# Last quarter of a selective scan: nine of 64 state products made by TensorE and ScalarE instead of VectorE and GpSimd, on one Trainium2 core

## The chip, the cores and the metric

One core of a Trainium2 chip runs the whole program in one launch. The metric is the device time of one launch in microseconds (us); below, a time is the median of repeated launches, and the span is what the profiler shows of one launch from its first to its last instruction. The engines have their own instruction queues and are tied together by semaphores: TensorE (PE in the rows, PEld its weight loads), VectorE (DVE), ScalarE (ACT), GpSimd (POOL) and SyncE (SP), which issues most DMAs.

## The reference

A layer of attention, a mixture of experts, then a bidirectional Mamba block on 4 sequences of 256 positions, and a gated feed-forward block. The change is in the Mamba block, of which this is the core:

```python
def step(h, inp):
    dt_t, B_t, C_t, x_t = inp
    dA = jnp.exp(dt_t[..., None] * A)
    h = dA * h + (dt_t * x_t)[..., None] * B_t[:, None, :]
    y = jnp.einsum('bds,bs->bd', h, C_t)
    return (h, y)
```

There are DI = 512 channels d and DS = 16 states s. The output y is then multiplied with silu(z) and goes through a projection.

## The kernel before

The Mamba block (function `mamba`) treats four segments: a direction (two forward, then two backward) times half of the 1024 positions (HALF = 512, two sequences). A segment has 64 steps (SSTEP), in two pairs of channel blocks with 32 steps (PSTEP) each, so there are 256 steps and eight pairs, numbered 0 to 7. A step is one block of 128 channels (two blocks take turns) and one state s, over 512 positions. Steps are named here by their place in the pair: step 17 of pair 6 is n = 6 * 32 + 17 = 209. The last segment is pairs 6 and 7.

A step goes through five engines:

- GpSimd multiplies u with the row B for two steps at once (line 2119, "uB"), three such pairs ahead at most (UPAIRS).
- ScalarE writes exp(dt * A) into a PSUM bank (lines 2222 and 2223, tile `da` or `side`). Which bank a step gets is worked out by `banks`: three banks `da`, and the bank `S1` (tile name `side`) where `spare` says that nothing else needs it. In the last segment `spare` is true throughout, so four banks go round, and step n's exp waits until step n-4 has been read.
- VectorE runs the recurrence (`tensor_tensor_scan`): in place in the bank (line 2339), or, where GpSimd makes the product, into one of four buffers hS (line 2336).
- The product with the row C is made by VectorE (line 2238, 20 of 32 steps, called V steps here), one step behind the scan, or by GpSimd (line 2129, 12 of 32 steps, P steps: 1, 3, 5, 8, 10, 12, 15, 17, 19, 22, 24, 26). GpSimd's product of step m stands in its queue behind the uB of steps m+4 and m+5. It has three output buffers, and waits until TensorE has added the product three before.
- TensorE adds the products in PSUM (`ya0`, `ya1`; lines 2360 and 2364). In pairs 0 to 6 the sum is kept turned, so an add is four transposes of 128x128; a copy (line 1739), `sum_back` and VectorE's gate (line 2250) follow at step 4 of the next pair. In pair 7 the sum isn't turned, and an add is one matmul of 512 columns (two passes).

All five queues are written out by hand and are strictly in order. Beside the steps each engine has a side program (`side_tensor`, `side_scalar`, `side_vector`), a generator that yields the step at which its next piece is due: `side.advance(step)` issues all that is due. On TensorE the step given is the index of the add in the order of `summed` (a P step's add comes four places late) plus AHEAD = 2. In the last segment TensorE's side program has the dt matmuls of block 2 (due 2) and 3 (due 17), their sums (`sum_tensor`, due 10 and 22), the output projection of the segment before (due 18 and 30) and the first half of its own (due 48). ScalarE's has abs and relu (due 9 and 23), exp (11, 24), ln (12, 25) and the copy of dt (`keep_dt`, 20 and 31), then eight table copies (34 to 48), each issued after the exp of that step. `dt_tensor` of block 3 waits for `keep_dt` of block 2, and `sum_tensor` for the ln of its block, since they share banks.

At a segment's beginning ScalarE loads another table, makes silu(z) and loads the first table again (lines 1775 and 1933). After the last scan VectorE makes three table pieces (line 2020), the two gates of pair 7, five more pieces and the two output sums (line 2025); TensorE makes the second half of the projection (line 1624) as the gates come.

Of the kernel before, what the change touches and what calls it, by code (L numbers as in the profile page):

```python
# [24 lines left out]
P = 128  # L25
# [5 lines left out]
HALF = 512  # L31
# [29 lines left out]
DB = DI // P  # L61
# [1213 lines left out]
UPAIRS, CBUF, PBUF, DABUF, HBUF = 3, 4, 3, 3, 4  # L1275
# [31 lines left out]

def on_pool(n):

    return n % PSTEP % 7 in (1, 3, 5) and n % PSTEP < PSTEP - LATE  # L1310


def pool_steps(n):

    full, part = divmod(n, PSTEP)
    return full * sum(on_pool(i) for i in range(PSTEP)) + sum(on_pool(i) for i in range(part))


def vector_steps(n):
    return n - pool_steps(n)  # L1320
# [74 lines left out]
def mamba(c, g, dram, wt, ws, acc, hh, hl, xn, sc, first_weights):  # L1395
# [25 lines left out]
    s_dd, s_yt, s_yb = map(sem, "dd yt yb".split())  # L1421
    s_da, s_ub, s_sc, s_hv, s_hp, s_av, s_ap, s_sk, s_g, s_om, s_oa = map(
# [3 lines left out]
    with ExitStack() as ctx:  # L1426
# [18 lines left out]
        def read(e, n):  # L1445

            if on_pool(n):
# [180 lines left out]

        def dt_tensors(e, k):
# [14 lines left out]
        def side_tensor(e, seg):  # L1644
            k = seg + 1
# [86 lines left out]
        def copy_sum(e, pair, b):  # L1732
# [3 lines left out]
            e.wait_ge(s_ap, pool_steps(last))  # L1736
            if pair:
# [268 lines left out]
        def side_scalar(e, seg):  # L2006
            own = first_scalar(e) if seg == 0 else middle_scalar(e, seg) if seg < NSEG - 1 else last_scalar(e)
            return in_turn(sums_scalar(e, seg), own)
# [57 lines left out]
        with nc.Block() as block:  # L2066
# [25 lines left out]
            def _(e):  # L2092
# [11 lines left out]
                for r in range((STEPS + LATE) // 2):  # L2104
# [17 lines left out]
                    for m in (2 * r - LATE, 2 * r - LATE + 1):  # L2122
                        if m >= 0 and on_pool(m):
# [5 lines left out]
                            e.tensor_tensor(hP[:, k % PBUF, :], hS[:, k % HBUF, :], RC[:, row % CROWS, :],  # L2129
# [3 lines left out]
            def _(e):  # L2133
# [66 lines left out]
                for n in range(STEPS):  # L2200
# [13 lines left out]
                    elif BANK[n] == DABUF:  # L2214
                        e.wait_ge(s_dtc, DB * (seg + 1) + 1)
                    to, first = by_seq(states[BANK[n]][:, :]), 0 if seg < 2 else SEQ - 1
# [3 lines left out]
                    stays = past is not None and on_pool(past) and place(past)[0] // 2 == seg // 2  # L2220
# [6 lines left out]
                    side.advance(n % SSTEP)  # L2227
                side.finish()

            @block.vector  # L2230
            def _(e):
# [9 lines left out]
                def gate(pair, b):  # L2241

                    last, seg, d = (pair + 1) * PSTEP, pair // 2, 2 * (pair % 2) + b
                    if pair == LASTPAIR:
                        e.wait_ge(s_av, vector_steps(last - 1 + b))
                        e.wait_ge(s_ap, pool_steps(last))
                    else:
# [71 lines left out]
                for n in range(STEPS):  # L2319
# [12 lines left out]
                    if on_pool(n):  # L2332
                        k = pool_steps(n)
                        if k >= HBUF:
                            e.wait_ge(s_hp, k - HBUF + 1)
# [5 lines left out]
                    if n and not on_pool(n - 1):  # L2341
# [565 lines left out]
```

## Time and profile before

| | us |
|---|---|
| median of 3 launches | 930.74 (930.12 to 931.51) |
| profiled launch | 922.39 |
| span in the profile | 920.7 |
| PE, DVE, ACT, POOL busy | 759.4, 762.6, 541.6, 658.8 |
| VectorE's last product ends | 843.4 |

The scans run from about 430 to 843 us of the span. The profiled launch was itself 8.4 us shorter than the median; differences worked out on its span are added to the median. An engine that is busy for nearly all of a stretch isn't yet its bound: what each waits for, and how short the waits are, has to be read from the timelines.

### The profile page before, as it was taken

To read this page: it belongs to the slowest core of one execution; us is meant where nothing else is said; L and a number is where in the kernel's file an instruction comes from. 1 tells how busy PE (TensorE), PEld (TensorE's weight loads), DVE (VectorE), ACT (ScalarE), POOL (GpSimd) and SP (SyncE) were. 2 spreads that over 40 slices of the span, in tenths; PEclk is the share of its full clock that TensorE was granted. 3 is DMA by queue.
4 is the path that set the end of the run, shared out by engine and by line. 5 is a ranking of instruction groups with operands and counts; after the bars stand their busy time and mean duration, and the time that the engine had idled before them with its cause. 6 is when DMAs were issued, how large, how long until landed. Compare 5 with 4: busy or idle time off the path is not lost. (4 is left out here: it accounts for less than half of the span.)

```text
span 920.7 us, 13477 instructions
## 1 busy us (share of the span) xinstructions
PE 759.4 (82%) x3802; PEld 492.4 (53%) x3802; DVE 762.6 (83%) x1261; ACT 541.6 (59%) x1303; POOL 658.8 (72%) x454
## 2 busy tenths in 40 slices
PE   4889977899999994797879579787879766877998
PEld 2466654466666662344555455445645554422786
DVE  3588867678889985848989999999999999999843
ACT  1588855444444442476777887677775785652332
POOL 3177853477777883229999989999999999995000
PEclk9899999799999998898989799999999988799999
DMA  4000008599879844414565565656557665552001
GB/s 117 1 1 1 0 1 336 216 414 328 300 275 355 298 146 154 128 47 134 156 169 185 160 153 152 190 158 175 142 163 192 155 173 155 164 157 58 1 1 46
DMA packets 67347, 141.77 MB, mean 154 GB/s; under 512 B 12688, under 2 KB 23312, under 8 KB 65104
## 3 DMA queue, kind: packets, MB, share of 16 engines
q1 hardware_dynamic: 56432, 117.62, 42.2%
q0 software_dynamic: 6048, 18.59, 5.7%
q10 hardware_dynamic: 4800, 4.78, 1.6%
q8 instruction: 28, 0.46, 0.2%
q14 instruction: 39, 0.32, 0.1%
HBM read 129.92 MB, written 11.04 MB: 153 GB/s over the span
## 5 line engine op out<-in xcount | busy, mean ns | idle before, releaser
L2119 POOL TENSOR_TENSOR uB<-u,rows_B 128x1024 f32<-128x1024 f32 x127 | 297.9, 2354 | 0.0
L2339 DVE TENSOR_TENSOR_SCAN da<-da,uB 128x512 f32<-128x512 f32 x145 | 175.1, 1220 | 11.8 <-ACT da L2223 9.9
L2364 PE MATMUL ya<-ident,hV 128*128 128x128 f32 x560 | 96.2, 302 | 49.7 <-DVE hV L2238 49.6
L2129 POOL TENSOR_TENSOR hP<-hS,rows_C 128x512 f32<-128x512 f32 x96 | 121.7, 1268 | 8.3 <-PE ya L2364 3.9
L2364 PEld LDWEIGHTS ya<-ident,hV 128*128 128x128 f32 x560 | 71.4, 153 | 102.1 <-DVE hV L2238 76.3
L2336 DVE TENSOR_TENSOR_SCAN hS<-da,uB 128x512 f32<-128x512 f32 x86 | 103.6, 1204 | 6.2 <-issue 2.6
L1232 PE MATMUL gups<-wring,xT 128*128 128x448 f32 x252 | 105.8, 542 | 0.0
L1140 POOL DMA_INDIRECT xg<-x_rows,li x63 | 71.9, 1142 | 38.7 <-issue 14.6
L2238 DVE TENSOR_TENSOR hV<-da,rows_C 128x512 f32<-128x512 f32 x145 | 96.8, 668 | 0.7 <-DMA rows_C<-bc_rows 0.7
L1147 POOL DMA_INDIRECT y_rows<-y,yi x63 | 72.1, 1145 | 21.4 <-issue 17.1
L2222 ACT ACTIVATE da<-zero 128x2 f32<-128x2 f32 x145 | 25.0, 173 | 102.0 <-DVE hV L2238 101.1
L1069 DVE SCALAR_TENSOR_TENSOR lutw<-eq,lutb,lutw 128x865 f32<-128x865 bf16 x75 | 83.5, 1113 | 0.0
L2223 ACT ACTIVATE da<-dt,fm_A 128x510 f32<-128x510 f32 x123 | 81.7, 674 | 0.0
L372 POOL TENSOR_TENSOR prob<-prob,ri 128x1024 f32<-128x1024 f32 x32 | 60.6, 1893 | 22.9 <-DVE ri L535 22.9
L2223 ACT ACTIVATE da<-dt,bm_A 128x510 f32<-128x510 f32 x108 | 71.6, 674 | 0.0
L606 ACT ACTIVATE prob<-sps,mx 128x256 f32<-128x256 f32 x128 | 58.9, 478 | 7.3 <-DVE mx L531 7.2
L1232 PEld LDWEIGHTS gups<-wring,xT 128*128 128x128 f32 x252 | 47.8, 191 | 27.5 <-issue 24.1
L2364 PEld LDWEIGHTS ya<-ident,hP 128*128 128x128 f32 x336 | 44.0, 150 | 23.1 <-issue 21.1
L2364 PE MATMUL ya<-ident,hP 128*128 128x128 f32 x336 | 54.6, 288 | 0.0
L881 ACT ACTIVATE y<-yps 128x256 f32<-128x256 f32 x63 | 24.2, 384 | 47.7 <-DMA y_rows<-y,yi 31.9
L531 DVE TENSOR_REDUCE mx<-sps 128x4 f32<-128x1024 f32 x32 | 39.1, 1221 | 13.8 <-PE sps L436 12.8
L1487 PE MATMUL side<-raw,conv_diag 128*128 128x512 f32 x72 | 38.6, 619 | 5.1 <-ACT side L1703 5.1
(429 smaller groups left out, 1733.6 us busy)
## 6 DMA issues: line engine op xcount, KB each, us to landing
rows_B<-bc_rows SPq DMA_DIRECT2D x128, 256.0 KB, 3.6
rows_C<-bc_rows SPq DMA_DIRECT2D x128, 256.0 KB, 4.3
wring<-in_moe_own SPq DMA_DIRECT2D x31, 704.0 KB, 5.8
wring<-in_moe_two SPq DMA_DIRECT2D x16, 1024.0 KB, 14.3
rows_sum<-y_rows SPq DMA_DIRECT2D x6, 512.0 KB, 8.3
lut_i<-in_lut_idx SPq DMA_DIRECT2D x1, 2160.0 KB, 8.4
x<-in_x SPq DMA_DIRECT2D x4, 256.0 KB, 3.4
x_rows<-xnw ACTq DMA_DIRECT2D x1, 1024.0 KB, 14.4
```

The costliest lines, as they stand in the source:

```text
L372: e.tensor_tensor(prob[:, u % NP, :, :], prob[:, u % NP, :, :], ri[:, u, :].unsqueeze(2).broadcast_to([P, GROUPS, SEQ]), ALU.mult).then_in ...
L1069: e.scalar_tensor_tensor(part, eq[:, n % 4, 0:LCH], g.lutb[:, l:l + 1], part, ALU.mult, ALU.add).then_inc(s_ad, 1)
L1140: e.indirect_dma_start(xg[:, t % XG, :], None, dram["xs"], bass.IndirectOffsetOnAxis(ap=li[:, t:t + 1], axis=0)).then_inc(s_xg[t % XG], 16)
L1147: e.indirect_dma_start(dram["ys"], bass.IndirectOffsetOnAxis(ap=ri[:, t:t + 1], axis=0), y[:, t % YB, :], None).then_inc(s_sc[t % YB], 16)
L1232: mm = e.matmul(gups[:, t % 2, 0:BOTH], xT[:, t % 2, k * P:(k + 1) * P], both[k], start=k == 0, stop=k == KC - 1)
L2119: e.tensor_tensor(uB[:, r % UPAIRS, :, :], u[:, d:d + 2, :], RB[:, r % BROWS, :].unsqueeze(1).broadcast_to([P, 2, HALF]), ALU.mult).then_i ...
L2129: e.tensor_tensor(hP[:, k % PBUF, :], hS[:, k % HBUF, :], RC[:, row % CROWS, :], ALU.mult).then_inc(s_hp, 1)
L2223: e.activation(to[:, :, rest], by_seq(dt[:, d, :])[:, :, rest], ACT.Exp, scale=ws[seg // 2].A[:, d, r % DS:r % DS + 1]).then_inc(s_da, 2 i ...
L2238: e.tensor_tensor(hV[:, k % CBUF, :], states[BANK[n]][:, :], RC[:, r % CROWS, :], ALU.mult).then_inc(s_hv, 1)
L2336: e.tensor_tensor_scan(hS[:, k % HBUF, way], a[:, way], uB[:, r % UPAIRS, b, way], 0.0, ALU.mult, ALU.add).then_inc(s_sc, 1)
L2339: e.tensor_tensor_scan(a[:, way], a[:, way], uB[:, r % UPAIRS, b, way], 0.0, ALU.mult, ALU.add).then_inc(s_sc, 1)
L2364: mm = e.matmul(ya[n % 2][:, part], at[:, part], g.ident[:, :], start=False, stop=False, is_transpose=True, skip_group_check=True)
```

## The change

A third kind of step, A, is made by neither VectorE nor GpSimd. Its scan goes to an hS buffer. TensorE turns the four 128x128 parts into the bank S1 (`turn_state`), ScalarE copies them out with a per-partition scale, the turned C (`scale_state`: four activations of 128x128), and TensorE adds the result: with one matmul in pair 6, whose sum is turned already, with four transposes in pair 7. The kinds of all steps are now strings. Pairs 0 to 5 keep theirs. Pair 6 has A at 10, 14, 19, 25, P at 1, 3, 5, 8, 12, 16, 18, 21, 23, 27 and 18 V steps; pair 7 has A at 3, 9, 13, 19, 23, P at 1, 5, 7, 11, 15, 17, 21, 24, 26, 28 and 17 V steps.

B and C are turned once, near the end of the third segment (`turn_rows`, `keep_rows`, due 62). Since S1 is now used for turning, `spare` is true in the last segment only for steps 0 to 6. TensorE's side program is advanced, in all eight pairs, by the step at whose turn the add is issued rather than by its index in the order. The buffer of B and C moves (`bcr`), the hS count covers P and A steps, and both gates of pair 7 wait for A adds too.

```diff
-UPAIRS, CBUF, PBUF, DABUF, HBUF = 3, 4, 3, 3, 4
+UPAIRS, CBUF, PBUF, DABUF, HBUF, TBUF = 3, 4, 3, 3, 4, 2
+SCALED, ADDED = 3, 6
+KINDS = ["VPVPVPVVPVPVPVVPVPVPVVPVPVPVVVVV"] * (2 * NSEG - 2) + ["VPVPVPVVPVAVPVAVPVPAVPVPVAVPVVVV",
+                                                                "VPVAVPVPVAVPVAVPVPVAVPVAPVPVPVVV"]
...
     seg, m = divmod(n, SSTEP)
     if seg == NSEG - 1:
-        return True
+        return m < 7
...
-    order = []
-    for n in range(pair * PSTEP, (pair + 1) * PSTEP):
-        if not on_pool(n):
-            order.append(n)
-        if n - LATE >= pair * PSTEP and on_pool(n - LATE):
-            order.append(n - LATE)
+    first, order = pair * PSTEP, []
+    for n in range(first, first + PSTEP + LATE):
+        if n < first + PSTEP and not on_pool(n):
+            order.append((n, False))
+        if n - LATE >= first and on_pool(n - LATE):
+            order.append((n - LATE, True))
+        if n - ADDED >= first and turned(n - ADDED):
+            order.append((n - ADDED, True))
...
+        def turn_rows(e):
+            yield 62
+            e.wait_ge(s_bcc, NSEG)
+            e.wait_ge(s_dtc, DB * (NSEG - 1) + 1)
+            for q in range(HALF // P):
+                mm = e.transpose(S1[:, q * 2 * DS:(q + 1) * 2 * DS], sc.bcr[:, q * P:(q + 1) * P],
+                                 g.ident[0:2 * DS, 0:2 * DS])
+            mm.then_inc(s_tb, 1)
+        def keep_rows(e):
+            yield 62
+            e.wait_ge(s_tb, 1)
+            e.activation(sc.bT[:, :, :].rearrange("p q s -> p (q s)"), S1[:, 0:HALF // P * 2 * DS],
+                         ACT.Copy).then_inc(s_bt, 1)
+        def turn_state(e, n):
+            k, i = kept_steps(n), turned_steps(n)
+            e.wait_ge(s_sc, n + 1)
+            if i:
+                e.wait_ge(s_hs, i)
...
+            for q in range(HALF // P):
+                part = slice(q * P, (q + 1) * P)
+                mm = e.transpose(S1[:, part], hS[:, k % HBUF, part], g.ident[:, :])
+            mm.then_inc(s_ht, 1)
+        def scale_state(e, n):
+            i, at = turned_steps(n), DS + n // 2 % DS
+            e.wait_ge(s_ht, i + 1)
+            if i >= TBUF:
+                e.wait_ge(s_at, i - TBUF + 1)
+            for q in range(HALF // P):
+                part = slice(q * P, (q + 1) * P)
+                a = e.activation(sc.hT[i % TBUF][:, part], S1[:, part], ACT.Identity, scale=sc.bT[:, q, at:at + 1])
+            a.then_inc(s_hs, 1)
...
                     side.advance(n % SSTEP)
+                    if n >= SCALED and turned(n - SCALED):
+                        scale_state(e, n - SCALED)
...
-                    if n // PSTEP == LASTPAIR:
+                    if (n // PSTEP == LASTPAIR) != is_turned:
...
-                        if on_pool(n):
+                        if turned(n) and not late:
+                            turn_state(e, n)
+                        elif turned(n):
+                            k = turned_steps(n)
+                            e.wait_ge(s_hs, k + 1)
+                            add(n, sc.hT[k % TBUF][:, :], s_at, True)
+                        elif on_pool(n):
...
-                        side.advance(pair % 2 * PSTEP + i + AHEAD)
+                        side.advance((n + (0 if not late else LATE if on_pool(n) else ADDED)) % SSTEP + AHEAD)
```

## Rows read from the trace of the kernel before

**Rows 1.** Stretches: length, busy PE, PEld, DVE, ACT, POOL; clock, DMA share, GB/s.
```profile
750.00:800.00 50.00, 36.59 (x169) 25.14 (x168) 49.83 (x57) 30.26 (x66) 49.75 (x28) 0.80 0.60 161
800.00:850.00 50.00, 39.05 (x82) 13.88 (x80) 48.96 (x58) 20.73 (x45) 40.36 (x23) 1.00 0.42 116
```

**Rows 2.** Groups of instructions, 730 to 850 us: busy, mean ns of one.
```profile
L2119 POOL TENSOR_TENSOR uB<-u,rows_B 128x1024 f32<-128x1024 f32 x34 | 79.6, 2350 | 0.0
L2129 POOL TENSOR_TENSOR hP<-hS,rows_C 128x512 f32<-128x512 f32 x26 | 32.9, 1265 | 0.2 <-DVE hS L2336 0.2
```

**Rows 3.** VectorE's timeline: start, us, line (idle before, releaser).
```profile
756.77 1.20 DVE L2336 TENSOR_TENSOR_SCAN hS<-da,uB 128x512 f32<-128x512 f32 x1
757.89 0.66 DVE L2238 TENSOR_TENSOR hV<-da,rows_C 128x512 f32<-128x512 f32 x1
758.47 1.22 DVE L2339 TENSOR_TENSOR_SCAN side<-side,uB 128x512 f32<-128x512 f32 x1
...
829.84 1.22 DVE L2336 TENSOR_TENSOR_SCAN hS<-da,uB 128x512 f32<-128x512 f32 x1 [0.61 <-ACT da L2223]
```

**Rows 4.** GpSimd's timeline, same stretch.
```profile
827.40 4.65 POOL L2119 TENSOR_TENSOR uB<-u,rows_B 128x1024 f32<-128x1024 f32 x2
```

**Rows 5.** ScalarE's timeline: scaled 128x128 activations, the copy of dt, two exps.
```profile
482.56 0.97 ACT L1766 ACTIVATE conv_diag<-ident,bm_cvw 128x128 f32<-128x128 f32 x3
...
769.50 0.58 ACT L1811 ACTIVATE dt<-side 128x512 f32<-128x512 f32 x1
...
783.41 1.28 ACT L2223 ACTIVATE da<-dt,bm_A 128x510 f32<-128x510 f32 x2
```

**Rows 6.** ScalarE's timeline where the last segment begins.
```profile
738.10 0.17 ACT L2222 ACTIVATE da<-zero 128x2 f32<-128x2 f32 x1 [0.31 <-DVE hV L2238]
...
738.90 1.28 ACT L1775 ACT_TABLE_LOAD   x1
```

**Rows 7.** VectorE and TensorE there.
```profile
744.24 1.23 DVE L2339 TENSOR_TENSOR_SCAN da<-da,uB 128x512 f32<-128x512 f32 x1 [1.09 <-ACT da L2223]
...
736.35 0.66 PE L2364 MATMUL ya<-ident,hV 128*128 128x128 f32 x4 [1.06 <-DVE hV L2238]
```

**Rows 8.** TensorE's timeline in pair 6, around the dt matmul of block 3.
```profile
769.71 1.06 PE L2364 MATMUL ya<-ident,hP 128*128 128x128 f32 x4
770.57 1.92 PE L1582 MATMUL side<-dtr,wdt 128*128 128x512 f32 x2
...
774.14 0.60 PE L2364 MATMUL ya<-ident,hP 128*128 128x128 f32 x4
774.57 1.02 PE L1602 MATMUL side<-sz,w_o 128*128 128x512 f32 x2
```

**Rows 9.** A stretch of 6 us in pair 6, columns as above.
```profile
768.00:774.00 6.00, 5.20 (x16) 3.49 (x17) 6.00 (x8) 3.67 (x8) 6.00 (x4) 0.55 0.59 153
```

**Rows 10.** VectorE and TensorE at the start of pair 7.
```profile
798.01 1.28 DVE L2250 TENSOR_TENSOR sz<-ya,sz 128x512 f32<-128x512 f32 x2
...
798.84 1.10 PE L1723 MATMUL ya<-xi,skip_diag 128*128 128x512 f32 x2 [0.57 <-DVE sz L2250]
799.77 1.88 PE L2360 MATMUL ya<-hV,ident 128*128 128x512 f32 x4
```

**Rows 11.** The tail, VectorE and TensorE.
```profile
845.16 1.28 DVE L2250 TENSOR_TENSOR sz<-ya,sz 128x512 f32<-128x512 f32 x2
...
843.78 1.02 PE L2360 MATMUL ya<-hP,ident 128*128 128x512 f32 x2
844.64 1.02 PE L2360 MATMUL ya<-hV,ident 128*128 128x512 f32 x2
845.91 3.70 PE L1624 MATMUL side<-sz,w_o 128*128 128x512 f32 x8 [0.24 <-DVE sz L2250]
```

**Rows 12.** GpSimd waits in segment 2, and VectorE later in that segment.
```profile
652.09 1.28 POOL L2129 TENSOR_TENSOR hP<-hS,rows_C 128x512 f32<-128x512 f32 x1 [1.10 <-PE ya L2364]
...
673.93 1.22 DVE L2336 TENSOR_TENSOR_SCAN hS<-da,uB 128x512 f32<-128x512 f32 x1 [0.61 <-issue]
```

More of the change, by code:

```diff
@@ L1305, in finish, with kind, turned, turned_steps @@
         self.advance(NEVER - 1)
+def kind(n):
+    return KINDS[n // PSTEP][n % PSTEP]
 def on_pool(n):
-    return n % PSTEP % 7 in (1, 3, 5) and n % PSTEP < PSTEP - LATE
+    return kind(n) == "P"
+def turned(n):
+    return kind(n) == "A"
 def pool_steps(n):
-    full, part = divmod(n, PSTEP)
-    return full * sum(on_pool(i) for i in range(PSTEP)) + sum(on_pool(i) for i in range(part))
+    return sum(on_pool(i) for i in range(n))
+def turned_steps(n):
+    return sum(turned(i) for i in range(n))
+def kept_steps(n):
+    return pool_steps(n) + turned_steps(n)
 def vector_steps(n):
-    return n - pool_steps(n)
+    return n - kept_steps(n)
+KEPT = [n for n in range(STEPS) if kind(n) != "V"]
+TURNED = [n for n in range(STEPS) if turned(n)]
 def place(n):
@@ L1644, in side_tensor, with own_tensor @@
         def side_tensor(e, seg):
+            rows = [turn_rows(e)] if seg == NSEG - 2 else []
+            return in_turn(*rows, own_tensor(e, seg))
+        def own_tensor(e, seg):
             k = seg + 1
@@ L1736, in copy_sum @@
             e.wait_ge(s_ap, pool_steps(last))
+            if turned_steps(last):
+                e.wait_ge(s_at, turned_steps(last))
             if pair:
@@ L2007, in side_scalar @@
             own = first_scalar(e) if seg == 0 else middle_scalar(e, seg) if seg < NSEG - 1 else last_scalar(e)
-            return in_turn(sums_scalar(e, seg), own)
+            rows = [keep_rows(e)] if seg == NSEG - 2 else []
+            return in_turn(sums_scalar(e, seg), own, *rows)
         def split_vector(e, i):
@@ L2215, in _ @@
                         e.wait_ge(s_dtc, DB * (seg + 1) + 1)
+                        if seg == NSEG - 2:
+                            e.wait_ge(s_bt, 1)
                     to, first = by_seq(states[BANK[n]][:, :]), 0 if seg < 2 else SEQ - 1
                     rest = slice(1, SEQ) if seg < 2 else slice(0, SEQ - 1)
-                    stays = past is not None and on_pool(past) and place(past)[0] // 2 == seg // 2
+                    stays = past is not None and kind(past) != "V" and place(past)[0] // 2 == seg // 2
                     if not stays:
@@ L2340, in _ @@
                                              ALU.mult, ALU.add).then_inc(s_sc, 1)
-                    if n and not on_pool(n - 1):
+                    if n and kind(n - 1) == "V":
                         product(n - 1)
@@ L2437, in _ @@
                     begun = 0
-                    for i, n in enumerate(summed(pair)):
+                    for n, late in summed(pair):
                         if n % 2 == begun and begun < 2:
```

22 lines of the change are left out of this document (15 added, 7 removed).

## The prediction

> **What bounds the kernel now.** I read the stretches first, then the groups, then the timelines of the last segment engine by engine. In the stretches VectorE and GpSimd are both full: 49.83 and 49.75 of 50 us [rows 1]. The timelines tell which is late. A scan follows the last after 1.12 us and a product adds 0.58 [rows 3]; a uB takes 2.33 and a GpSimd product 1.23, from start to start, 2.35 and 1.265 each by themselves [rows 2]. At 829.84 VectorE sat idle for 0.61 us. The view names ScalarE, but the uB that this scan (step 24 of pair 7) needs is the first of two from 827.40, and it ended at 829.73 [rows 3, 4]. So from about 778 us on GpSimd is the last to be ready, by a little: the idle times of VectorE from there to the end are 0.17, 0.34, 0.61, 0.18 and 0.1 us, 1.4 in all, of which one row stands. If GpSimd alone got lighter, 1.4 us would be gained and no more, since VectorE's own queue is full behind it.
>
> ScalarE and TensorE have time left in total (20.7 to 39 of 50 us busy [rows 1]), and this is what the change spends. But they are queues in order, and ScalarE's exp stands in the same queue as the new copies. So the question is what each new piece stands in front of.
>
> **What goes.** VectorE loses 2 products in pair 6 and 3 in pair 7: 5 x 0.58 = 2.9 us. GpSimd loses 5 products before its last uB, 6.2 us, which is more than VectorE loses, so its lead grows and the 1.4 us of idle time go too, together -4.3 us. Next late is VectorE itself. The number of scans stays.
>
> **The fourth bank goes.** From step 7 of pair 6 step n's exp waits for step n-3. When n-3 is a V step and n-2 isn't, the time from the product's end to scan n is 1.05 us, and zero column plus exp take 0.11 + 0.67 + 0.07 = 0.85. ScalarE has only 0.2 us to spare there, once per two or three steps; between, it has some 1.4 us. By itself that costs nothing. It does move everything in ScalarE's side program later by up to a step.
>
> **A scale** is four activations of 128x128. The nearest row has three of them in 0.97 us, 0.29 apart [rows 5], so four hold ScalarE for 1.16 us. Bounds are 0.15 to 0.39 each, 0.6 to 1.6 in all. I take 1.16: same shape, same kind of scale, another source. It fits the gap of 1.4 us if TensorE has turned the state in time. Where it hasn't, ScalarE stands still in front of the next exp. This decides the result, so I place each one. Times count from the end of a named product.
>
> *Step 10 of pair 6.* TensorE now issues `sum_tensor` of block 2 (due 10) right behind the add of step 9, ahead of the turn. It waits for the ln behind step 12's exp, which, with three banks, waits for product 9: 0.8 (exp) + 0.5 (ln) = 1.3, sum 0.86, add of step 5 0.43, turn 0.6: 3.3. Scale to 4.5, exp of 14 to 5.3. VectorE wants step 14 at 3.9. Cost 1.4 us.
>
> *Step 19 of pair 6.* `dt_tensor` of block 3 (due 17) now stands behind the add of step 15. It waits for `keep_dt`, behind step 20's exp. Before, with four banks and one add later in the order, the copy began at 769.50 and the matmul followed the add before it without a gap, at 770.57 [rows 5, 8]. Now step 20's exp waits for product 17, which VectorE ends about 772.0: exp to 772.8, copy to 773.4. TensorE stands from about 769.1 to 773.4, and behind it are dt matmul, add of 12, an output matmul, add of 10, add of 17, an output matmul, and only then the turn of 19. At the higher clock these are 0.86 + 0.43 + 0.86 + 0.86 + 0.43 + 0.86 + 0.6 = 4.9 us, at the lower one at first (dt matmul 1.92, add 1.06 [rows 8]) about 7.0. Turned at 778.3 to 780.4, scaled 1.16 later, exp 0.8: step 23 can begin at 780.3 to 782.5, where VectorE wants it at 777.1. Cost 3.3 to 5.4; I take 4.4, because in the rows the clock came back some 4 us after the work got dense [rows 8, 9].
>
> A rule is weighed here. The clock fell to 0.55 of full in a stretch of pair 6 in which TensorE was busy for 5.2 of 6 us, mostly with transposes [rows 9], and was 1.00 throughout pair 7, where adds are matmuls [rows 1]. The Trainium skill ("TensorE: Matmul & The Clock Gate", Part 4: PE-mode transpose) says that transposes don't count as work for the clock as matmuls do. By this rule the turns that are added would not hold the clock up in pair 6, and the upper end, 5.4, would hold; the trace agrees as far as the stretches go.
>
> *End of pair 6.* `sum_tensor` of block 3 (due 22) stands behind the add of 20 and waits for the ln behind step 25's exp. The add of step 16 is behind it, GpSimd's product 23 waits for that add (three buffers), and the uB of steps 28 and 29 waits behind the product. By the same counting exp 25 is 0.35 late and scan 28 another 0.9: 1.25 us (0 to 2.5).
>
> *Step 3 of pair 7.* The gates start TensorE's first skip; the rows have 0.83 us from gate to skip, 0.93 to the first add, and two adds of 0.86 [rows 10]. Behind these now come the second skip and then the turn: turned 4.95 us after the gates' start. ScalarE reached it, after exp 6, long before, and exp 7 is behind it: 4.95 + 1.16 + 0.85 = 7.0 us. VectorE wants scan 7 at 1.2 + 3 x 1.12 + 0.58 = 5.2. Cost 1.8.
>
> *Steps 9, 13, 19, 23 of pair 7.* The turn ends 3.4 us after the scan's start, ScalarE is free at 3.2, and the next exp that waits is released at 4.65: no cost, but for a table copy in front (0.1 each, twice), and at 19 an output matmul of 0.86 before the turn: 0.6. Together 0.8. Steps 14 and 25 of pair 6 cost nothing: TensorE has caught up.
>
> **The turned rows.** `keep_rows` stands in ScalarE's queue after step 62's exp and the copy of dt, and waits for `turn_rows`, which stands behind the add that began at 736.35 [rows 7]. Turned 737.4, copied 737.7, where ScalarE is at 735.9 before. Behind it are two exps, a copy of z, and step 1's exp, before which ScalarE had 0.31 us to spare, then the table loads at 738.90 [rows 6]. They move to 740.4, and VectorE already waited at their end, 1.09 us at 744.24 [rows 7]. So all of it is paid: 1.5 us.
>
> **The tail.** GpSimd's product 28 ends before VectorE's last product, but its add is the last in TensorE's order, and both gates wait for it. Before: adds at 843.78 (step 26) and 844.64 (step 31), gate at 845.16, held by three table pieces [rows 11]. After, another add of 0.86 behind these: the gates at 846.5 on the same scale. The projection and the tables follow from there. Cost 1.35 us (0.9 to 1.4).
>
> **Pairs 0 to 5.** Only the order on TensorE changes: side work is issued one or two adds earlier. At the start of segment 2 GpSimd waited 1.10 us for an add [rows 12], since TensorE waited for ScalarE's copy. Two side pieces more now stand before the add of step 1, about 1.0 us, so GpSimd's wait grows by as much, and GpSimd is what VectorE waits for later there [rows 12]. The same pattern stands in segment 1. Against it, ScalarE gets TensorE's results earlier. Bounds -0.5 and 3; I take 1.5.
>
> **The sum:** -4.3 + 1.4 + 4.4 + 1.25 + 1.8 + 0.8 + 1.5 + 1.35 + 1.5 = +9.7 us. The span would go from 920.7 to 930.4 and the profiled launch from 922.39 to 932.1; added to the median, 930.74 + 9.7 = 940.4. With each cost at its lower bound it is 935, at its upper one 945.5.
>
> **Rivals.**
>
> *The gain arrives (faster).* If the turned states are ready before ScalarE needs them, in pair 6 too, only -4.3 and the tail are left: 927.8 us. It takes that the side program's waits on TensorE end before the turns are due, which the idle time of ScalarE speaks for (0.3 to 2 us at most exps) and the order of the queues speaks against. It decides at step 19: if scan 23 isn't late, this is the case.
>
> *Only the fixed costs.* TensorE's waits for keep_dt and ln cost little, but rows, gates and tail do as worked out: -4.3 + 1.5 + 1.8 + 0.8 + 1.35 = +1.15, 931.9 us.
>
> *Worse.* TensorE, slow in clock at the end of pair 6, is late for the copy of the sums (every add of 1.06 instead of 0.60), the gates stall by 2.5 us more, and pairs 0 to 5 cost 3: 946 us.
>
> A strict order on each engine is what all of this counts on. The Trainium skill ("Perfetto Trace Analysis", Per-engine timelines, TensorE) says that TensorE may only pull a weight load ahead, and that ScalarE and VectorE keep their order. By this rule no turn passes a waiting side matmul, and the forecast stands; in the trace of before every add stood behind its side matmul.
>
> **How the numbers follow.** Forecast 0.62, gain 0.18, fixed costs 0.10, worse 0.10. About 0.2% (1.9 us) is what a measurement of this kernel tells from no change. Faster 0.20, same 0.09, slower 0.71. The forecast's own range is 935 to 945; to leave out no more than 2 in 10, the range is 928.5 to 945.
>
> **What would show it.** In the changed kernel: VectorE's idle time in the last segment well above 1.4 us, with its longest piece (3 to 5 us) at step 23 of pair 6, and pieces of about 1.4 at step 14 and 1.8 at step 7 of pair 7, all ended by ScalarE's exp; ScalarE idle before its scales until TensorE's turn; TensorE idle before line 1582 until the copy of dt; GpSimd no longer busy throughout; 1.5 us more at the segment's beginning; gates 3 us after the last product. The forecast is wrong if ScalarE's scales never wait, or a scale takes under 0.8 us.

## The result and the profile after

The changed kernel takes 951.23 us (median of 4 launches, 947.96 to 955.68) where the kernel before takes 930.43 (929.78 to 931.51): a ratio of 1.0227 with a 95% interval of 1.0196 to 1.0258, 20.8 us slower. The direction was as forecast; the size wasn't: the forecast was 9.7 us, and its range ended at 945 us.

Two launches differ before the Mamba block's first scan, in code that no version here touches: it starts at 417.58 us of the span before, at 423.84 after, and between 410.96 and 433.61 in the experiments. From the first scan to the end of the span launches can be compared far better: 503.1 us before, 522.4 after, **+19.3 us**. Versions whose code is the same up to the last segment agree at its start to 0.7 us (the changed kernel and the three built on it with that code are late by 5.64 to 6.29 us there); on the way they differ by up to 1.4 us (2.49 and 3.93 at pair 4). So below, "late by" means later than in the kernel before, both counted from their own first scan. The profiled launch of after is 947.96 us with a span of 946.24; of its 25.6 us over the profiled launch before, 6.3 lie ahead of the first scan.

The page's busy time by engine, of the changed kernel:

```profile
PE 767.8 (81%) x3844; PEld 502.6 (53%) x3844; DVE 761.1 (80%) x1256; ACT 551.9 (58%) x1336; POOL 653.0 (69%) x450
```

No engine got much more to do. Its costliest groups (busy and mean ns, then idle time just before and what ended most of it) show what changed:

```profile
L2204 POOL TENSOR_TENSOR hP<-hS,rows_C 128x512 f32<-128x512 f32 x92 | 117.0, 1272 | 28.0 <-PE ya L2445 18.6
L2417 DVE TENSOR_TENSOR_SCAN hS<-da,uB 128x512 f32<-128x512 f32 x96 | 115.7, 1205 | 20.0 <-ACT da L2300 12.2
```

GpSimd stood idle for 18.6 us because TensorE hadn't added its product of three before. The stretches that answer to [rows 1] (length, busy PE, PEld, DVE, ACT, POOL; clock, DMA share, GB/s):

```profile
750.00:800.00 50.00, 31.67 (x130) 21.58 (x128) 39.16 (x43) 31.12 (x69) 40.40 (x22) 0.73 0.53 148
800.00:850.00 50.00, 39.89 (x134) 21.18 (x135) 44.26 (x50) 30.64 (x73) 42.06 (x22) 0.86 0.49 134
```

VectorE and GpSimd, full before, are at 39 and 40 of 50 us in the first of them, and TensorE and ScalarE at 32 and 31: what bounds the last segment now is waiting. VectorE's timeline says where (start, us, line, tiles, idle before and its releaser):

```profile
757.28 1.23 DVE L2420 TENSOR_TENSOR_SCAN da<-da,uB 128x512 f32<-128x512 f32 x1 [1.96 <-ACT da L2300]
...
778.48 1.22 DVE L2417 TENSOR_TENSOR_SCAN hS<-da,uB 128x512 f32<-128x512 f32 x1 [2.92 <-ACT da L2300]
...
797.50 1.22 DVE L2417 TENSOR_TENSOR_SCAN hS<-da,uB 128x512 f32<-128x512 f32 x1 [5.88 <-ACT da L2300]
...
807.87 1.23 DVE L2420 TENSOR_TENSOR_SCAN da<-da,uB 128x512 f32<-128x512 f32 x1 [2.26 <-POOL uB L2194]
...
822.79 1.29 DVE L2330 TENSOR_TENSOR sz<-ya,sz 128x512 f32<-128x512 f32 x2 [1.28 <-PE ya L1820]
...
829.62 1.22 DVE L2417 TENSOR_TENSOR_SCAN hS<-da,uB 128x512 f32<-128x512 f32 x1 [1.58 <-ACT da L2300]
...
870.74 1.29 DVE L2330 TENSOR_TENSOR sz<-ya,sz 128x512 f32<-128x512 f32 x2 [1.36 <-PE ya L2441]
```

In order: the table loads of the segment's beginning, scans 14, 23 and 28 of pair 6, the gates and scan 7 of pair 7, and the gates of the tail. These are the places that the prediction named, but for the first gates. TensorE's timeline shows the cause of the two longest:

```profile
773.08 2.05 PE L1614 MATMUL side<-u,ident 128*128 128x512 f32 x2 [0.77 <-ACT side L1881]
774.91 1.06 PE L2445 MATMUL ya<-ident,hP 128*128 128x128 f32 x4
775.77 0.83 PE L1683 MATMUL side<-ident,hS 128*128 128x128 f32 x4
...
780.34 1.11 PE L2445 MATMUL ya<-ident,hV 128*128 128x128 f32 x4 [2.87 <-DVE hV L2317]
...
788.02 2.05 PE L1608 MATMUL side<-dtr,wdt 128*128 128x512 f32 x2 [3.73 <-ACT dt L1885]
789.86 1.06 PE L2445 MATMUL ya<-ident,hP 128*128 128x128 f32 x4
790.71 1.91 PE L1628 MATMUL side<-sz,w_o 128*128 128x512 f32 x2
...
801.11 2.04 PE L1614 MATMUL side<-u,ident 128*128 128x512 f32 x2 [3.34 <-ACT side L1881]
802.95 1.06 PE L2445 MATMUL ya<-ident,hP 128*128 128x128 f32 x4
```

Three times TensorE waits for ScalarE's side work, with a turn or a late add behind, and the work behind each wait runs at half speed: 2.05 us for a side matmul that takes 1.02 elsewhere in the same segment, in the kernel before too (its `sum_tensor`, line 1588, at 759.54). It isn't the wait just ahead that slowed it each time: the add at 780.34 is slow already, before the wait of 3.73 us began. ScalarE in turn stands before its scaled copies, with the next exp behind them:

```profile
776.64 1.14 ACT L1694 ACTIVATE h_turned<-side,rows_turned 128x128 f32<-128x128 f32 x4 [3.10 <-PE side L1683]
...
787.30 0.58 ACT L1885 ACTIVATE dt<-side 128x512 f32<-128x512 f32 x1
...
795.65 1.14 ACT L1694 ACTIVATE h_turned<-side,rows_turned 128x128 f32<-128x128 f32 x4 [6.59 <-PE side L1683]
```

And GpSimd's product 23 of pair 6 follows the add that ended at 804.01:

```profile
804.18 1.27 POOL L2204 TENSOR_TENSOR hP<-hS,rows_C 128x512 f32<-128x512 f32 x1 [9.53 <-PE ya L2445]
```

### The profile page after: what moved, and what is told of

Its sections match the earlier page's. It is cut to its first block and busy times, and to the rows that moved or that the text cites. A ratio compares the mean times of both kernels' runs of the same rounds, so it can differ in the third digit from the quotient of the medians.

```text
span 946.2 us, 13602 instructions
## 1 busy us (share of the span) xinstructions
PE 767.8 (81%) x3844; PEld 502.6 (53%) x3844; DVE 761.1 (80%) x1256; ACT 551.9 (58%) x1336; POOL 653.0 (69%) x450
## 5 line engine op out<-in xcount | busy, mean ns | idle before, releaser
L2420 DVE TENSOR_TENSOR_SCAN da<-da,uB 128x512 f32<-128x512 f32 x150 | 181.4, 1220 | 15.6 <-ACT da L2300 10.1
L2204 POOL TENSOR_TENSOR hP<-hS,rows_C 128x512 f32<-128x512 f32 x92 | 117.0, 1272 | 28.0 <-PE ya L2445 18.6
L2417 DVE TENSOR_TENSOR_SCAN hS<-da,uB 128x512 f32<-128x512 f32 x96 | 115.7, 1205 | 20.0 <-ACT da L2300 12.2
L2445 PE MATMUL ya<-ident,hV 128*128 128x128 f32 x552 | 93.4, 300 | 30.0 <-DVE hV L2317 29.8
L2317 DVE TENSOR_TENSOR hV<-da,rows_C 128x512 f32<-128x512 f32 x150 | 99.8, 666 | 0.7 <-DMA rows_C<-bc_rows 0.7
L2300 ACT ACTIVATE da<-dt,bm_A 128x510 f32<-128x510 f32 x123 | 81.2, 679 | 0.0
```

The lines of the kernel that those rows point to most:

```text
L2204: e.tensor_tensor(hP[:, k % PBUF, :], hS[:, kept_steps(m) % HBUF, :], RC[:, row % CROWS, :], ALU.mult).then_inc(s_hp, 1)
L2300: e.activation(to[:, :, rest], by_seq(dt[:, d, :])[:, :, rest], ACT.Exp, scale=ws[seg // 2].A[:, d, r % DS:r % DS + 1]).then_inc(s_da, 2 i ...
L2317: e.tensor_tensor(hV[:, k % CBUF, :], states[BANK[n]][:, :], RC[:, r % CROWS, :], ALU.mult).then_inc(s_hv, 1)
L2417: e.tensor_tensor_scan(hS[:, k % HBUF, way], a[:, way], uB[:, r % UPAIRS, b, way], 0.0, ALU.mult, ALU.add).then_inc(s_sc, 1)
L2420: e.tensor_tensor_scan(a[:, way], a[:, way], uB[:, r % UPAIRS, b, way], 0.0, ALU.mult, ALU.add).then_inc(s_sc, 1)
L2445: mm = e.matmul(ya[n % 2][:, part], at[:, part], g.ident[:, :], start=False, stop=False, is_transpose=True, skip_group_check=True)
```

## The experiments

The last number of each is the time from the first scan to the end of the span: 503.1 before, 522.4 after. For kernels launched once no interval is given; their times stand beside those of the kernel before on the same chip, and the time from the first scan is the surer number. It comes from one launch too: with equal code the gates of pair 7 alone differed by up to 1.8 us (below).

**1. The order of side work alone, in the kernel before.**

```diff
-                        side.advance(pair % 2 * PSTEP + i + AHEAD)
+                        side.advance((n + (LATE if on_pool(n) else 0)) % SSTEP + AHEAD)
```

> The kernel before with one part of the change alone: TensorE's side program is advanced by the step at whose turn an add is issued, not by its index. All products stay where they were. In the changed kernel's trace the scans of pairs 0 to 5 are 5.2 us late against before (counted from the first scan of the block). Theory (the order on TensorE does it: side work stands one or two adds earlier, P adds come later, GpSimd waits for its buffers): the same 5 us late at the first scan of pair 6, and some more in pairs 6 and 7, so 935 to 938 us. Rival (the 5 us come of moved buffers or of another launch's memory traffic): within 1 us of before, 930.5.

Measured: 924.22 against 919.43 us, ratio 1.0048 (1.0020 to 1.0077); 508.8 us, +5.7. It is late by 1.0 at pair 2, 2.3 at pair 4, 3.7 at pair 5 and 5.0 at the end of pair 5, where the changed kernel is late by 5.24. So nearly all that the change loses in pairs 0 to 5 is this one line. The waits of TensorE between 420 and 760 us (total, times, longest), before:

```profile
PE side L1487 <- ACT side L1703: 5.1, 4, 1.5
PE side L1582 <- ACT dtr L1791: 1.3, 2, 0.7
PE side L1588 <- ACT side L1807: 1.1, 2, 0.6
```

and with the line changed:

```profile
PE side L1487 <- ACT side L1703: 11.0, 5, 3.5
PE side L1588 <- ACT side L1807: 10.4, 4, 4.0
...
PE side L1582 <- ACT dtr L1791: 5.4, 2, 2.8
```

TensorE reaches the side matmuls before ScalarE has what they need, 26.8 us of waiting for these three instead of 7.5, and the adds stand behind. GpSimd's timeline of the same kernel has the longest of what follows:

```profile
609.29 1.29 POOL L2129 TENSOR_TENSOR hP<-hS,rows_C 128x512 f32<-128x512 f32 x1 [1.23 <-PE ya L2364]
650.14 1.27 POOL L2129 TENSOR_TENSOR hP<-hS,rows_C 128x512 f32<-128x512 f32 x1 [2.87 <-PE ya L2364]
```

The second is the 1.10 us of [rows 12]. In all, GpSimd waited for adds for 8.9 us in seven places instead of 3.9 in five.

**2. The changed kernel with side work advanced by the index in the order again.** Turns aren't counted in the index.

```diff
+                    made = -1
...
+                        made += late or not turned(n)
...
-                        side.advance((n + (0 if not late else LATE if on_pool(n) else ADDED)) % SSTEP + AHEAD)
+                        side.advance(pair % 2 * PSTEP + max(made, 0) + AHEAD)
```

> The changed kernel with the old rule for TensorE's side program (index of the add; a turn counts as no add). Theory: pairs 0 to 5 run as before, 5.2 us come back; in pair 6 the waits of 3, 5.9 and 2.8 us stay, since the side matmuls still stand ahead of the turns of steps 10 and 19. Some 945 us (943 to 947). Rival (the order is beside the point): 951.

Measured: 927.63 against 919.43, ratio 1.0094 (1.0065 to 1.0124); 513.8, +10.7. Pairs 0 to 5 are back (late by 0.1). VectorE's idle times before pair 6 and before scan 14, then in pair 7 (timeline):

```profile
736.32 1.23 DVE L2420 TENSOR_TENSOR_SCAN side<-side,uB 128x512 f32<-128x512 f32 x1 [2.29 <-ACT side L2300]
...
764.09 1.22 DVE L2417 TENSOR_TENSOR_SCAN hS<-da,uB 128x512 f32<-128x512 f32 x1 [2.29 <-ACT da L2300]
...
803.51 1.29 DVE L2330 TENSOR_TENSOR sz<-ya,sz 128x512 f32<-128x512 f32 x2 [3.15 <-PE ya L1820]
```

The wait at scan 23 is gone, which I hadn't expected. TensorE's timeline:

```profile
773.63 1.10 PE L1608 MATMUL side<-dtr,wdt 128*128 128x512 f32 x2 [0.55 <-ACT dt L1885]
774.56 0.60 PE L1683 MATMUL side<-ident,hS 128*128 128x128 f32 x4
```

The dt matmul of block 3 is ahead of the turn of step 19 here too, but three adds (of steps 12, 10 and 17) now come before it, and the output matmuls after the turn. It waits 0.55 us instead of 3.73, runs at full speed, and the turn follows at once. So a turn behind the dt matmul doesn't make the stall by itself; the matmul must also come long before its input. The turned rows come later here, and cost 2.3 before pair 6 instead of 0.6.

**3. Three banks, nothing else, in the kernel before.**

```diff
-        return True
+        return m < 7
```

> The kernel before with three state banks instead of four from step 7 of pair 6, nothing else. Theory: ScalarE's exp keeps up by itself; its side program comes up to a step later, so TensorE stands before the dt matmul of block 3 for some us, but no turn is behind it: 1 to 4 us, 932 to 934. Rival 1 (the loss of the bank is most of the whole loss): 938 or more. Rival 2 (it costs nothing): 930.5.

Measured: 917.33 against 919.43, ratio 0.9972 (0.9941 to 1.0002); 503.0. Late by -0.1 throughout. The loss of the fourth bank costs nothing by itself, as the prediction had it, and what I expected here for waits of scans was wrong.

**4. The changed kernel with later dues for TensorE's side work in the last segment,** so that the turns of steps 10 and 19 come first.

```diff
-                yield 10
+                yield 12
...
-                yield 17
+                yield 20
...
-                yield 18
-                yield from out_tensor(e, seg - 1, 0, 18)
-                yield 22
+                yield 20
+                yield from out_tensor(e, seg - 1, 0, 20)
+                yield 27
```

> The changed kernel with TensorE's side pieces of pair 6 due later, behind the turns they stood in front of: sum of block 2 at 12 instead of 10, dt of block 3 at 20 instead of 17, projection at 20 instead of 18, sum of block 3 at 27 instead of 22. No work is added or left out. Theory (side matmuls that wait for ScalarE hold up the turns and GpSimd's adds): the idle times of VectorE at steps 14, 23 and 28 of pair 6 (2.9, 5.9, 2.3 us) go, all but one us or so: 940.5 us (939 to 943). Rival (the copies that ScalarE has more, or TensorE's clock, hold up the exps wherever the turns stand): 948 or more.

Measured: 927.33 against 919.43, ratio 1.0081 (1.0049 to 1.0113); 512.3, +9.2, so 10.1 less than the changed kernel. Four numbers take away the idle times before scans 23 and 28 and the gates, and leave 0.80 of the 2.92 before scan 14. One new wait came: VectorE's output sum now stands ahead of its matmuls.

```profile
785.29 0.69 DVE L2100 TENSOR_TENSOR acc<-side,acc 128x512 f32<-128x512 f32 x1 [2.13 <-PE side L1628]
```

**5. Number 4 with the old order in the first three segments,** the turned rows due at 59 and VectorE's output sum due at 27.

```diff
+                    made = -1
...
+                        own = (n + (0 if not late else LATE if on_pool(n) else ADDED)) % SSTEP
+                        made += 1
-                        side.advance((n + (0 if not late else LATE if on_pool(n) else ADDED)) % SSTEP + AHEAD)
+                        side.advance((own if seg == NSEG - 1 else pair % 2 * PSTEP + made) + AHEAD)
```

> As the kernel with the later side pieces in pair 6, and besides: TensorE's side program by the old index in pairs 0 to 5, the turning of B and C issued three adds earlier (59 instead of 62), VectorE's output sum at step 27 instead of 24. Counted from the first scan of the block to the end, before takes 503.1 us and that kernel 512.3. Theory: pairs 0 to 5 give back 5.0, the turned rows 1.5 (up to 3.3), the output sum 2.1: 503.5 to 504.5 us. Rival (each of these waits only covers another): above 507.

Measured: 932.49 beside 931.5; 504.5, +1.4. So 17.9 of the 19.3 us went with places in queues; all nine turned states are still made. At scan 27 of pair 6 it is ahead by 1.9 us and at the pair's end by 1.3; then the gates take 2.2 and scan 7 of pair 7 another 1.7.

**6. Number 5 with the places of pair 7 moved** (turned states at 7, 11, 15, 19 and 23, none at 3).

```diff
-"VPVAVPVPVAVPVAVPVPVAVPVAPVPVPVVV"
+"VPVPVPVAVPVAVPVAVPVAVPVAPVPVPVVV"
```

> The kernel above with the five A steps of pair 7 at 7, 11, 15, 19, 23 instead of 3, 9, 13, 19, 23. Theory (the turn of step 3 stands behind the second skip, which waits for a gate, and ScalarE's exp of step 7 behind its copy): the 1.6 us idle at step 7 go and nothing comes in their place: 1.3 to 1.8 us less than the kernel above. Rival (any first A step of the pair meets TensorE's work from the pair's start): less than 0.5.

Measured: 928.5 beside 931.5; 503.1, 1.4 less than number 5. The 1.58 us before scan 7 are gone, which shows that the turn of step 3 behind the skips made them (0.39 us came new, before scan 19).

**7. Number 6 without GpSimd's product at step 28.**

```diff
-"VPVPVPVAVPVAVPVAVPVAVPVAPVPVPVVV"
+"VPVPVPVAVPVAVPVAVPVAVPVAPVPVVVVV"
```

> The kernel above with step 28 of pair 7 back on VectorE, so four products fewer on VectorE than before instead of five. Theory: the last add of GpSimd's product, behind which both gates stood for 1.4 us, is gone, one product of 0.58 us comes back: 0.8 us less; from the first scan 501 us or a little less, 2 us less than before, ratio 0.998. Rival (the gates are held by the adds of TensorE in any case): 0.6 us more than the kernel above.

Measured over 12 launches: 928.64 against 931.5, ratio 0.9974 (0.9953 to 0.9994), so 0.6 to 4.4 us faster; 500.9, 2.2 us less than the kernel before. The idle time of the tail's gates is gone: from VectorE's last product to the end it is 77.3 us again, as before, instead of 78.8. Against it the product of step 28 comes back to VectorE (0.6 us), so 0.9 of the 2.2 us by which it leads number 6 are the edit's, as expected; the other 1.3 are not. The gates at step 4 of pair 7 waited 2.44 us there and 0.67 here, in the same code: TensorE had its last side matmuls and adds of pair 6 at half speed there and mostly not here. VectorE's idle times in the last segment, all that its timeline marks up to the last scan:

```profile
754.68 1.23 DVE L2420 TENSOR_TENSOR_SCAN da<-da,uB 128x512 f32<-128x512 f32 x1 [1.09 <-ACT da L2300]
...
807.72 1.29 DVE L2330 TENSOR_TENSOR sz<-ya,sz 128x512 f32<-128x512 f32 x2 [0.67 <-PE ya L1820]
...
830.92 1.22 DVE L2417 TENSOR_TENSOR_SCAN hS<-da,uB 128x512 f32<-128x512 f32 x1 [0.39 <-ACT da L2300]
...
836.95 1.22 DVE L2417 TENSOR_TENSOR_SCAN hS<-da,uB 128x512 f32<-128x512 f32 x1 [0.26 <-ACT da L2300]
```

The idea of the change works, for about half of the 4.3 us that the prediction had as its gain, and in a launch where the gates cost little.

**8 and 9. Number 1 with `AHEAD` 1, and with `AHEAD` 0, instead of 2.** This asks whether the new order costs only because side work comes early.

> The kernel before with the step rule for TensorE's side program, but AHEAD 1 instead of 2, so that side work is issued one step later than in the kernel with the rule alone (5.7 us late from the first scan to the end). Theory (side work one or two adds too early delays the adds that GpSimd's buffers wait for): most of it comes back, 503.5 to 505 us from the first scan. Rival (it is the irregular order itself, not how early it is): 507 or more.

> The kernel before with the step rule for TensorE's side program and AHEAD 0. With AHEAD 2 it is 5.7 us late from the first scan to the end, with AHEAD 1 it was 4.4. At AHEAD 0 the step given equals the old index plus 2 at nearly every add. Theory (side work that comes even one add early puts it ahead of adds that GpSimd waits for): 503 to 504 us from the first scan, GpSimd waits for adds 4 us as before. Rival (the order is worse in itself): 506 or more.

Measured: 936.23 beside 931.5 with 1, and 939.20 beside 933.62 with 0; 507.5 (+4.4) and 506.9 (+3.8). I had expected most of the 5.7 us back and got 1.3 and 1.9. With 0, TensorE's waits for the side work fall back to what they were before, but another grew, from 8.2 us before to

```profile
PE ya L1746 <- ACT y_turned L1739: 16.5, 5, 6.0
```

GpSimd's waits for adds are 5.3 us, near the 3.9 before, and yet it is late by 2.0 at pair 6, by 3.7 at its end and by 4.6 at step 4 of pair 7. So "earlier" is half an explanation: with 0 the step given is nearly the old one, and most of the loss is still there. Which of the places that still differ makes it, no run shows.

**10. The changed kernel with TensorE kept busy through its wait:** 5 matmuls of 128x512 more, in two passes each, into a bank that is written again, ahead of the dt matmul of block 3.

```diff
+                e.wait_ge(s_dtc, DB * seg + 2)
+                e.wait_ge(s_zc, DB * (seg + 1))
+                for _ in range(5):
+                    e.matmul(S0[:, :], g.ident[:, :], sc.wo[:, 0:2, :].rearrange("p q n -> p (q n)"), start=True, stop=True)
                 dt_tensor(e, seg, 3)
```

> The changed kernel with five matmuls of 512 columns more, whose results nobody uses, on TensorE ahead of the dt matmul of block 3 in pair 6, where it stood idle for 3.73 us. They change nothing in what waits for what; TensorE is busy instead of idle there. In the changed kernel VectorE idles 5.88 us at step 23, with the granted clock low after the wait. Theory (the wait and the low clock after it both count): the matmuls behind the wait run at full clock, the turn of step 19 comes 1.5 to 2 us earlier, idle time at step 23 3.5 to 4.5 us. Rival (the clock doesn't matter, or the extra matmuls come late themselves): 5.5 or more.

Measured: 951.24 beside 933.62; 519.9, 2.5 less than the changed kernel. The idle time before scan 23 is 4.70 instead of 5.88, which is neither the 3.5 to 4.5 of the theory nor the 5.5 of its rival. TensorE's timeline says why:

```profile
789.61 5.61 PE L1727 MATMUL side<-w_o,ident 128*128 128x512 f32 x10
795.05 1.02 PE L1608 MATMUL side<-dtr,wdt 128*128 128x512 f32 x2
795.91 0.60 PE L2449 MATMUL ya<-ident,hP 128*128 128x128 f32 x4
796.35 1.02 PE L1628 MATMUL side<-sz,w_o 128*128 128x512 f32 x2
```

The copy of dt ended at 793.41, and the dt matmul began 1.6 us later, behind the added matmuls; without them it would have begun 0.14 us after the copy, as in the changed kernel, so it began 1.5 late. But from there to the end of step 19's turn it is 4.9 us, where the changed kernel takes 7.6. The clock is 2.7 us of the 5.88, and 1.5 of that was spent on the overrun. The granted clock was 0.50 from 785.09 on, as in the changed kernel at that place, and rose while the added matmuls ran.

**11. Number 7 with every scaled copy made twice.** The second set writes the same values.

```diff
+    s_ft2 = sem("ft2")
...
+            for again in range(2):
...
+                if not again:
+                    a.then_inc(s_ft2, 1)
+                    e.wait_ge(s_ft2, i + 1)
```

> The fastest kernel so far (500.9 us from the first scan) with each of the nine scaled copies made twice into the same buffer, so ScalarE holds for 2.2 instead of 1.1 us each; nothing is left out. Theory (a copy is free only as far as it fits ScalarE's gap of 1.4 us; at 1.1 us it nearly does): VectorE idles some 0.5 to 1.1 us at most of the nine, 505 to 510 us from the first scan. Rival (ScalarE has slack enough in total, so the size of the copy doesn't matter): 501 to 502.

Measured: 943.48 beside 933.62; 507.8, 6.9 more than number 7. The doubled set takes 2.3 us instead of 1.14. Nine of them add 10.4 us to ScalarE's queue and 6.9 come out at the end. In pair 6 little is felt, in pair 7 most, the longest piece being

```profile
842.54 1.22 DVE L2422 TENSOR_TENSOR_SCAN hS<-da,uB 128x512 f32<-128x512 f32 x1 [2.36 <-ACT da L2305]
```

So a set of 1.14 us fits ScalarE's gaps in number 7, and there isn't room for a second one in the last pair.

**12. Number 10 with transposes for the matmuls:** 20 transposes of 128x128. The prediction had weighed a rule by which these wouldn't hold the clock.

```diff
+                for _ in range(5):
+                    for q in range(HALF // P):
+                        e.transpose(S0[:, q * P:(q + 1) * P], g.ident[:, :], g.ident[:, :])
```

> The changed kernel with 20 transposes of 128x128 (the identity by itself, into a bank that is written again) in front of the dt matmul of block 3, where e9_busy has 5 matmuls of 128x512 in two passes each, 10 passes. Nothing is left out. Theory A, that transposes don't hold TensorE's clock up as matmuls do: the granted clock stays at its low level, the 20 transposes take about 5 x 1.06 = 5.3 us, the dt matmul 1.9 to 2.05 us (1.02 in e9_busy), and the idle time of VectorE before step 23 of pair 6 is 5.9 (as in the changed kernel) plus the 1 to 1.5 us by which they run past the copy of dt: 6.5 to 7.4 us. Theory B, that any dense work brings the clock back: dt matmul 1.02 us, idle time 4.7 or less (4.70 in e9_busy), since the transposes at the higher clock (0.6 us for four) also end earlier. From the first scan to the end 519 to 520 us by B, 522.5 to 524 by A.

Measured: 931.60 beside 921.11; 518.9, 3.5 less than the changed kernel and 0.1 below what Theory B had. TensorE:

```profile
771.56 3.52 PE L1728 MATMUL side<-ident 128*128 128x128 f32 x20
775.50 1.10 PE L1608 MATMUL side<-dtr,wdt 128*128 128x512 f32 x2 [0.42 <-ACT dt L1890]
776.43 0.60 PE L2450 MATMUL ya<-ident,hP 128*128 128x128 f32 x4
```

and VectorE, before scan 23 and scan 28 of pair 6:

```profile
782.37 1.22 DVE L2422 TENSOR_TENSOR_SCAN hS<-da,uB 128x512 f32<-128x512 f32 x1 [3.26 <-ACT da L2305]
791.38 1.23 DVE L2425 TENSOR_TENSOR_SCAN da<-da,uB 128x512 f32<-128x512 f32 x1 [0.90 <-ACT da L2304]
```

The 20 transposes end before the copy of dt, and the matmul behind them runs at full speed: the granted clock was 0.50 when they began and 1.00 from 773.94 on. Theory B holds. Without the low clock the wait before scan 23 is 3.26 us, the lower end of what was forecast. Here `sum_tensor` of block 3 also ran in 1.10 us, although it came after a wait of 3.34 as in the changed kernel (2.04 there), and scan 28 waited 0.90 instead of 2.26: a single wait of this length doesn't always bring the clock down.

## Why the prediction was wrong

Every move of the lateness along the changed kernel, beside the term of the sum:

| place | forecast | measured |
|---|---|---|
| pairs 0 to 5, order | 1.5 | 5.24 |
| turned rows, table loads | 1.5 | 1.55 |
| step 10 of pair 6 (scan 14) | 1.4 | 3.01 |
| step 19 (scan 23) | 4.4 | 5.88 |
| end of pair 6 (scans 28 and 29) | 1.25 | 2.59 |
| gates at the start of pair 7 | 0 | 1.37 |
| step 3 of pair 7 (scan 7) | 1.8 | 1.67 |
| steps 9, 13, 19, 23 of pair 7 | 0.8 | 0.40 |
| tail | 1.35 | 1.44 |
| what goes | -4.3 | -3.84 |
| sum | +9.7 | +19.3 |

The measured column is read off the starts of the scans, but for scan 23 and for scans 28 and 29 (2.26 and 0.33), where it is VectorE's idle time: there VectorE also makes other products than before, which moves the scans by some 0.6 us either way without a wait. "What goes" is what remains of the 19.3.

**Right.** What bounded the kernel, and what goes. Every place but the gates of pair 7, and the way it gets there: a turn or an add behind a side matmul that waits for ScalarE, shown by number 4 for steps 10 and 19 and the end of pair 6, by number 6 for step 3 and by number 7 for the tail. The fourth bank (number 3). A scale: forecast 1.16; the first takes 1.14 to its own end, holds ScalarE's next exp for 1.01, and begins 0.04 us after the turn. The turned rows, the tail and step 3 of pair 7 within 0.2 us.

**The first step that failed is "Pairs 0 to 5".** It read one wait, 1.10 us in [rows 12], added 1.0 us for two pieces in front of the add, did so for two segments, and took 1.5. The wait did grow by 1.8 (number 1). But the step looked at side work only as pieces that take time before an add. It didn't ask, for each piece, whether its input is ready one or two adds earlier. Where it isn't, TensorE stands, and that occurs all over the segments: 10.4 us behind the ln copy instead of 1.1, 11.0 behind the copy of the newest tap instead of 5.1 (number 1). An edit that touches 192 steps was costed at two of them. Here 3.7 of the 9.6 us that were missing went. That the order makes the loss is shown. That it does so by these waits is argued: with `AHEAD` 0 they are gone, and 3.8 us of loss stay (numbers 8 and 9). TensorE's waits have moved to the copy of the turned sum there; what makes the loss then stays open.

**The second is TensorE's clock behind its waits.** The terms of steps 10 and 19 and of the end of pair 6 count with matmuls of 0.86 and adds of 0.43, the higher level (2.4 GHz); only for step 19 did the prediction also work out the lower one, and took the middle. In the trace the granted clock was 0.50, which is 1.2 GHz, from 801 to 805 us, behind the wait of 3.34 us. Around the wait of 3.73 it was (columns as in [rows 1])

```profile
780.00:784.00 4.00, 2.80 (x12) 2.28 (x12) 4.00 (x5) 3.04 (x9) 2.43 (x2) 0.50 0.65 131
784.00:788.00 4.00, 0.28 (x2) 0.01 (x1) 4.00 (x6) 2.19 (x6) 4.00 (x3) 0.50 0.47 130
788.00:796.00 8.00, 7.98 (x22) 4.26 (x23) 3.62 (x4) 1.41 (x4) 6.56 (x4) 0.67 0.55 140
```

so it had fallen before, during the wait of 2.87 us that ended at 780.34, and it came back at 793.3, well into the work behind the wait. From the ln's end to the end of the turn or add that someone waits for, the prediction had 1.9 and 1.3 us; measured are 3.5 and 2.9. That is 1.6 us each. The term of step 10 is short by just this, the one of the end of pair 6 by 1.34. At step 19 the path from the dt matmul's start to the end of the turn was put at 4.9 (higher level) to 7.0 (lower); it took 7.6. For step 19 numbers 10 and 12 turn the argument into a measurement: with the engine kept busy the same path takes 4.9 and 5.0 us, and in number 12 the wait before scan 23 is 3.26 instead of 5.88. For the end of pair 6 number 12 bears it out, by chance: at the higher clock scan 28 waited 0.90. For step 10 it is read from the durations alone. Together the three terms are short by 1.6 + 1.5 + 1.3 = 4.4 us.

The rule that the prediction had weighed at this point, from the Trainium skill ("TensorE: Matmul & The Clock Gate", Part 4: PE-mode transpose), gave the upper end, which was the better number, but for a reason that doesn't hold here: in number 12 transposes alone brought the clock back. What stood ahead of the slow pieces in the changed kernel was each time a wait of TensorE; the same page calls the throttled clock the default, which activity releases (Part 1: The HAM clock gate). The low clock of [rows 9], where TensorE was busy, began at 766.6. In the 4 us up to 766 TensorE was busy for 1.20, at the higher clock:

```profile
762.00:766.00 4.00, 1.20 (x10) 0.73 (x8) 4.00 (x6) 1.63 (x5) 4.00 (x3) 1.00 0.41 146
```

So there too TensorE had waited before the clock fell; the transposes that the prediction weighed as the reason came behind the fall.

**The third is the gates of pair 7,** 1.37 us where the sum had none and the rival "Worse" had 2.5. TensorE is so late with pair 6's output matmuls and adds that the copy of the sum comes late. The same clock goes with it. In the last 15 us before the gates it was at 0.50 for about 3 us in the changed kernel and number 11 (VectorE waited 1.28 at the gates in both), in number 10 (0.63) and number 7 (0.67), for about 7 us in numbers 12 (2.00), 5 (2.16) and 6 (2.44), and for about 10 us in number 2 (3.15); in number 4 it never fell there, and the gates didn't wait. Numbers 6 and 7 have the same code up to there. No run sets the clock at this place and leaves the rest, so this is seen and not tested. In the kernel before the sum had slack enough not to show it.

3.7 + 4.4 + 1.4 = 9.5 us of the shortfall of 9.6. In the rest, "what goes" was 0.5 us less than forecast, and the small terms were together 0.4 lower. The rival "Worse" was the right one in kind, with pairs 0 to 5 at 3 and a slow TensorE at the gates, and still 5 us too low, since it let steps 10 and 28 stand at the higher clock. Its sum was short as well: 940.4 with 2.5 more at the gates and 1.5 more in pairs 0 to 5 is 944.4, not 946. The range ended at 945 because the bounds of the terms were too narrow. The upper bounds that the prediction states add up to 944.2 (it says 945.5), and they were passed in pairs 0 to 5 (5.24 against 3) and at step 19 (5.88 against 5.4) and just at the end of pair 6 (2.59 against 2.5), while step 10 had no bound and the gates no term. Most of them share one cause, TensorE late at the low clock, and came together.

## What to carry to other kernels

In a queue written out in order, a new piece costs what stands in front of it, not what it takes itself: list for each piece the wait ahead of it and who waits behind it, and give it a place where its input is just ready. Four changed dues were worth 10 us here and the places together 18, against a gain of 4 from the work moved. Price the work of TensorE in a stretch where it often waits at the low clock too, and not only behind the longest wait. When a rule of issue changes for all segments, cost it in all of them, or limit it to the segment that needs it.

## What the runs showed of the hardware

- A 128x512 matmul in two passes takes 1.02 us from start to end at the higher clock and 2.05 at the lower one; four 128x128 transposes take 0.60 and 1.06. Behind the wait of 3.73 us the add took 1.06 and the output matmul 1.91, but the clock was at 0.50 before that wait began; behind a wait of 3.34 both levels were seen, 2.04 in the changed kernel and 1.10 in number 12.
- Twenty transposes in front of a waiting matmul took 3.52 us and brought the clock back as ten matmul passes (5.61 us) did. The filler cost nothing where it ended before the wait did, and 1.5 us where it ended after it.
- Four ScalarE copies of 128x128 with a scale per partition, from PSUM, take 1.14 us together; two such sets with a semaphore wait between them take 2.3.
- Launches of the versions, whose code is the same up to there, part by up to 23 us before the block's first scan; from there on equal code differs by up to 1.4 us on the way and by at most 0.7 at the start of the last segment. The same instructions at the start of pair 7 still cost 0.67 or 2.44 us: TensorE had been at the low clock for about 3 us before them in the first case, for about 7 in the second.
